# First attention: two PSUM copies move from VectorE to ScalarE, and the value bias goes into the bias row

## The reference, cut to what matters

```python
Q = (layernorm(x) @ Wq.T + bq)   # 16 heads of 8
K = (ctx @ Wk.T + bk)
V = (ctx @ Wv.T + bv)
attn = softmax(Q K^T / sqrt(8))
x = x + tanh(g_xattn[0]) * ((attn @ V) @ Wo.T + bo)
```

## Time and profile before

| what | value |
|---|---|
| median of 3 runs | 825.99 us |
| span of the profiled execution, first to last instruction | 815.2 us |
| what lies around that span, against the median | 10.8 us |
| first attention, first to last instruction | about 10.3 to 206 us |
| busy over the span: PE, DVE, ACT, POOL | 775.3, 622.4, 558.0, 476.5 us |
| steps n = 2 to 28 by the starts of L787 | 42.37 to 183.98 us |

### The profile page before, as it was taken

The page is one execution under the profiler, slowest core; times in us unless marked ns, Lnnn a source line. Parts: engine busy times, 40 slices in busy tenths (PEclk is TensorE's granted clock), DMA queues, the critical chain, the costliest instruction groups (busy, mean ns, idle before and its releaser), DMA issues. The chain is left out here.

```text
span 815.2 us, 30741 instructions
## 1 busy us (share of the span) xinstructions
PE 775.3 (95%) x10664; PEld 637.5 (78%) x10669; DVE 622.4 (76%) x2406; ACT 558.0 (68%) x1125; POOL 476.5 (58%) x892
## 2 busy tenths in 40 slices
PE   4999999999999989999999999999999999889995
PEld 2777877787788868888888888888888888558884
DVE  4799999998677767888888888888888888734442
ACT  1688878886455568777777777777777777447762
POOL 6645777773011156577677686676776776605554
PEclk9999999999999999999999999999999999999998
DMA  8804999800200000000000000000000000023110
GB/s 223 303 3 149 264 241 235 195 1 3 72 1 0 0 1 2 3 7 7 7 0 7 7 7 7 7 0 7 7 7 7 0 7 7 10 68 91 33 33 19
DMA packets 56157, 41.65 MB, mean 51 GB/s; under 512 B 3897, under 2 KB 51651, under 8 KB 55856
## 3 DMA queue, kind: packets, MB, share of 16 engines
q1 hardware_dynamic: 52400, 36.39, 17.8%
q0 software_dynamic: 2272, 4.27, 1.6%
q10 hardware_dynamic: 1440, 0.40, 0.4%
HBM read 18.07 MB, written 23.44 MB: 51 GB/s over the span
## 5 line engine op out<-in xcount | busy, mean ns | idle before, releaser
L1654 PE MATMUL l_pv<-l_Z,l_probs 128*128 128x129 f32 x1024 | 164.1, 284 | 0.6 <-DVE l_acc L1161 0.6
L1654 PEld LDWEIGHTS l_pv<-l_Z,l_probs 128*128 128x128 f32 x1024 | 138.4, 191 | 20.0 <-DVE l_acc L1161 4.9
L1433 POOL TENSOR_TENSOR l_qk_lo<-w,l_qk_hi 128x512 f16<-128x512 f32 x132 | 148.9, 1160 | 1.7 <-ACT l_qk_hi L1511 1.3
L1161 DVE SCALAR_TENSOR_TENSOR x_sb<-l_pv,l_inv,x_sb 128x128 f32 (+1 forms) x256 | 89.8, 351 | 35.3 <-DVE l_inv L1148 6.9
L52 PE MATMUL l_tz<-M,cT 128*128 128x512 f16 x396 | 108.0, 382 | 0.2 <-DVE l_Z L1239 0.2
L1497 ACT ACTIVATE l_probs<-l_b 128x512 f32<-128x512 f32 x128 | 72.8, 594 | 50.5 <-PE l_b L1620 50.4
L1487 ACT ACTIVATE w<-l_qk_bank 128x512 f32<-128x512 f32 x129 | 77.0, 597 | 44.1 <-PE l_qk_bank L52 42.4
L520 DVE TENSOR_REDUCE n_shared<-fold_bank 128x4 f32<-128x512 f32 x128 | 87.3, 682 | 9.5 <-PE fold_bank L735 9.3
L1138 DVE TENSOR_REDUCE l_neg_max<-l_a 128x4 f32<-128x512 f32 x132 | 85.8, 681 | 2.6 <-PE l_a L1598 2.1
L1491 ACT ACTIVATE l_qk_hi<-w 128x512 f16<-128x512 f32 x129 | 80.5, 624 | 1.1
L1502 ACT ACTIVATE l_Z<-l_tz 128x512 f32<-128x512 f32 x128 | 76.7, 599 | 3.6
(11 more groups left out here) (291 smaller groups left out, 2266.4 us busy)
## 6 DMA issues: line engine op xcount, KB each, us to landing
expert_rows<-empty_row SPq DMA_DIRECT2D x8, 2178.0 KB, 24.6
x_sb<-expert_rows SPq DMA_DIRECT2D x36, 66.0 KB, 2.1
x_sb<-in_x SPq DMA_DIRECT2D x4, 512.0 KB, 6.9
ctx_sb<-in_ctx SPq DMA_DIRECT2D x4, 512.0 KB, 8.0
w<-in_L_ffn_w SPq DMA_DIRECT2D x1, 2048.0 KB, 9.2
w_raw<-in_L_ffn_gate_w SPq DMA_DIRECT2D x1, 1408.0 KB, 9.6
w_raw<-in_L_ffn_up_w SPq DMA_DIRECT2D x1, 1408.0 KB, 12.2
downT<-in_L_ffn_down_w SPq DMA_DIRECT2D x2, 512.0 KB, 4.3
```

The costliest lines, as they stand in the source:

```text
L1161: nc.vector.scalar_tensor_tensor(out=total, in0=O[:, h, 0:P], scalar=inv[:, j:j + 1], in1=total, op0=ALU.mult, op1=ALU.add).then_inc(summe ...
L1433: nc.gpsimd.tensor_tensor(qk_lo[:, w, m, Q * u:Q * u + Q].rearrange("p t n -> p (t n)"), qk[:, u, m, :], qk_hi[:, w, m, Q * u:Q * u + Q].r ...
L1654: last = nc.tensor.matmul(pv_bank[m % 2][:, h * (P + 1):(h + 1) * (P + 1)], probs[:, 2 * m + h, :], Z[:, w, 2 * m + h, :], start=True, sto ...
```

## The change

Two of VectorE's calls of each step go to ScalarE: `values(n)` (a PSUM read of 128 x 128, there with an addition of the bias, now a plain Copy) stands between the stacked queries and `projected_hi`, and `heads_transposed(n-2)` stands between the stacked keys and `sums_out`. The bias `bv` is no longer added to the values: it is loaded as a column, widened to a square, multiplied by `wo0` once on TensorE, and added to the bias row. The wait of `values` on qk_hi becomes a wait on `qk_done`.

```diff
-    k.bv0 = sb("bv0", [P, P])
+    k.bv0 = sb("bv0", [P, 1])
...
-                act.dma_start(k.bv0[:, :], on_all(A["L0_xattn_bv"])).then_inc(k.bias_landed, 16)
+                act.dma_start(k.bv0[:, :], column(A["L0_xattn_bv"])).then_inc(k.bias_landed, 16)
...
+        bv_wide = heads_out
...
                 def prime():
                     dve.wait_ge(k.bias_landed, BIAS_LOADS)
-                    nc.vector.tensor_scalar(bias_row[:, :], k.bo[:, 0, :], k.tg[:, 0:1], None, ALU.mult).then_inc(primed, 1)
+                    nc.vector.tensor_copy(bv_wide[:, :], k.bv0[:, :].broadcast_to([P, P])).then_inc(bv_ready, 1)
                     nc.vector.memset(neg_max[:, :, :], 0.0).then_inc(primed, 1)
                     nc.vector.memset(V[:, :, :, :], 1.0).then_inc(primed, 1)
+                    dve.wait_ge(bv_projected, 1)
+                    nc.vector.scalar_tensor_tensor(out=bias_row[:, :], in0=k.bo[:, 0, :], scalar=k.tg[:, 0:1], in1=b_bank[0][:, 0:P],
+                                                   op0=ALU.mult, op1=ALU.add).then_inc(primed, 1)
                     dve.wait_ge(primed, 7)
...
-                def values(n, s, beside):
-
-                    dve.wait_ge(v_done, n + 1)
-                    if beside:
-                        dve.wait_ge(qk_hi_ready, 2 * n + 8)
-                    nc.vector.tensor_tensor(V[:, s % 2, :, 0:D0], front_bank[:, P:2 * P].rearrange("p (h d) -> p h d", h=H),
-                                            k.bv0[:, :].rearrange("p (h d) -> p h d", h=H), ALU.add).then_inc(V_ready, 1)
-
...
-                def heads_transposed(n):
-                    dve.wait_ge(heads_moved, n + 1)
-                    nc.vector.tensor_copy(headsT[:, :], misc_bank[:, P:2 * P]).then_inc(headsT_ready, 1)
...
                         maxima(n + 1, s + 1, 2)
-                    if live(0):
-                        values(n, s, live(3))
                     if live(3):
                         projected_lo(n + 3, s + 3)
                     if live(1):
                         maxima(n + 1, s + 1, 3)
-                    if live(-2):
-                        heads_transposed(n - 2)
...
-                        pool.wait_ge(primed, 5)
+                        pool.wait_ge(primed, 7)
...
+                def values(n, s, beside):
+                    act.wait_ge(v_done, n + 1)
+                    if beside:
+                        act.wait_ge(qk_done, n + 4)
+                    if s == 0:
+                        act.wait_ge(primed, 7)
+                    nc.scalar.activation(V[:, s % 2, :, 0:D0], front_bank[:, P:2 * P].rearrange("p (h d) -> p h d", h=H), ACT.Copy).then_inc(V_ready, 1)
+
+                def heads_transposed(n):
+                    act.wait_ge(heads_moved, n + 1)
+                    nc.scalar.activation(headsT[:, :], misc_bank[:, P:2 * P], ACT.Copy).then_inc(headsT_ready, 1)
+
...
                         stacked(n + 2, s + 2, 0, q_stacked, stack_q)
+                    if live(0):
+                        values(n, s, live(3))
                     if live(3):
                         projected_hi(n + 3, s + 3)
...
                         stacked(n + 2, s + 2, 1, k_stacked, stack_k)
+                    if live(-2):
+                        heads_transposed(n - 2)
                     if live(-1):
                         sums_out(n - 1)
...
+                pe.wait_ge(bv_ready, 1)
+                nc.tensor.matmul(b_bank[0][:, 0:P], bv_wide[:, :], k.wo0[:, :], start=True, stop=True).then_inc(bv_projected, 1)
                 every_step(pe, step)
```

More of the change, by code:

```diff
@@ L434, in first_attention @@
         names = ("primed bn_done stats_ready norm_step xn_ready cT_hi_ready cT_ready bias_added T_moved T_hi_ready T_lo_ready qk_done qk_hi_ready "
-                 "qk_lo_ready v_done V_ready q_stacked k_stacked stack_q stack_k scored max_ready maxT_moved maxT_ready shifted "
+                 "qk_lo_ready v_done V_ready bv_ready bv_projected q_stacked k_stacked stack_q stack_k scored max_ready maxT_moved maxT_ready shifted "
                  "exp_done pv_done sums_ready sums_moved inv_ready heads_ready heads_moved headsT_ready projected x_done tokens_landed w_hi_ready").split()
         (primed, bn_done, stats_ready, norm_step, xn_ready, cT_hi_ready, cT_ready, bias_added, T_moved, T_hi_ready, T_lo_ready, qk_done, qk_hi_ready,
-         qk_lo_ready, v_done, V_ready, q_stacked, k_stacked, stack_q, stack_k, scored, max_ready, maxT_moved, maxT_ready, shifted,
+         qk_lo_ready, v_done, V_ready, bv_ready, bv_projected, q_stacked, k_stacked, stack_q, stack_k, scored, max_ready, maxT_moved, maxT_ready, shifted,
          exp_done, pv_done, sums_ready, sums_moved, inv_ready, heads_ready, heads_moved, headsT_ready, projected, x_done, tokens_landed, w_hi_ready) = map(sem, names)
```

## The result

The changed kernel takes **833.46 us** in the median of five runs (830.51 to 835.05), the kernel before 825.99 (824.17 to 828.72) beside it: a ratio of 1.0084, interval [1.0061, 1.0107]. It is slower, by 7.5 us where 2.8 were forecast.

A forecast was written before the change was run, and what follows sets the result against it. Chain B through ScalarE's queue was to set the first attention's period, 5.52 us against 5.38. Periods 2.9, jumps 0, ends -0.2 and start 0.1 sum to +2.8 on the median 825.99: 828.8 us, range 825.2 to 833.6.

The forecast's parts named there:

- the forecast's own: Range of the likeliest case, 827.3 to 831 us, from the copies' bounds and the ends; +1.7 to +5 had chance 0.45.
- the dear copies: Rival: values and heads cost 0.25 us each on ScalarE, chain B 5.70, +7.3 us, 833.3; chance 0.17.
- chain B: First attention, L744 through ScalarE's queue and VectorE back to L744: 5.20 us by itself, 5.52 with both copies.
- The five jumps: Periods where the hardware loop jumps back: 5.64 to 5.71 us as now, cost 0, between -0.2 and +0.7.
- Taken as 0.16 from one row of another stage: Each new ScalarE copy's spacing, from L1875; L647's 0.25 us was the upper end.
- 0.18 us: Slack in chain B between the stacked keys and L660, where the heads' 0.16 us was to fit.
- The rival in which VectorE was the bound: Faster: the 0.30 us idle before L787 vanishes in each step, 826.0 - 7.8 = 818.2 us; chance 0.20.
- 21 ordinary periods x 0.14 = +2.9: First attention's periods without a loop jump: each grows from 5.38 to 5.52 us, +2.9 in all.
- Ends of the stage: First attention before step 2 and behind step 28: pauses and shorter hand-overs, -0.2 us, between -0.7 and +0.3.
- 10.8 us around: Median 825.99 us against the profiled span of 815.2; gave a predicted span near 818.0.
- Start, +0.1: POOL waits for VectorE's longer `prime`, with batches TensorE needs queued behind: 0 to +0.2 us, taken as +0.1.
- the cover of 1.1 us for the new matmul: At the start, behind eight warm-up matmuls, TensorE idle until 15.08; uncovered it would cost about 0.5 us.

The follow-up runs named there:

- The extra copy in the chain and in the pause: Changed kernel plus one spare ScalarE Copy per step, behind the values (chain) or behind `transposed_hi` (pause): 836.62 us, 1.0123, and 831.33 us, 1.0068, against the kernel before.
- the swap: Changed kernel with VectorE doing `add_to_x` ahead of `transposed_lo`: 826.56 us, ratio 1.0004 to the kernel before.
- the values alone: Changed kernel with the copy of the transposed heads back on VectorE, only the values on ScalarE: 825.87 us, ratio 1.0001 to the kernel before.
- one copy with the chain cut: Changed kernel with the heads back on VectorE and `add_to_x` ahead of `transposed_lo`: 821.33 us, ratio 0.9940 to the kernel before.
- the heads alone: Kernel before with only the transposed heads' copy moved to ScalarE, values and bias on VectorE: 827.01 us, ratio 1.0022.

## Why the prediction came out as it did

The direction and the mechanism of the period were right, the size was too small: +2.8 us forecast, 5.2 in known places, 5.4 and 7.5 between the medians. 833.46 lies at the upper end of the range (825.2 to 833.6) and above the forecast's own (827.3 to 831). That it lies inside is in part luck: the range reached so far for the dear copies, which are not what happened.

- **The chain.** It was forecast that the period would be set by chain B through ScalarE's queue, 5.52 against 5.38. It is 5.56 in 19 of the 21 ordinary periods; the first two take 5.63 and 5.68, where before they took 5.48 and 5.49. The extra copy in the chain and in the pause shows the queue, the swap shows the chain's last link. The five jumps were forecast at 5.64 to 5.71 and came at 5.65 to 5.66 (before: 5.67 to 5.72).
- **The copies.** Taken as 0.16 from one row of another stage; their spacing is 0.15 and 0.16. The strided destination and the extra waits cost nothing that shows. The rival with dear copies has about the right total, 833.3, by a wrong mechanism.
- **The slack.** That one of the two copies would fit in 0.18 us is shown by the values alone. The rival in which VectorE was the bound falls with it: VectorE has 11.9 us less to do in 136, and gets it back as idle time before L505. The rule that it went by (the Trainium skill, Perfetto Trace Analysis, Optimizing Scalar/DVE Operations: offloading to ScalarE may make sense where VectorE is saturated) held here for one copy with the chain cut, 0.9940, and not for two with the chain closed, 1.0084.
- **The term mis-sized first: 21 ordinary periods x 0.14 = +2.9.** The rows gave +3.63 over all 26: 19 x 0.18 and 0.34 in the first two, less 0.13 in the jumps. Of the 0.18, ScalarE's own distance grew by 0.10, less than the 0.14 forecast. The forecast took L642 to L501 as 0.31, as the earlier trace rows have it; with both copies on ScalarE `transposed_hi` lasts 0.35 instead of 0.27, and the distance is 0.38. A spacing is what a row costs its own engine, a duration what it costs the engine that waits for it; the forecast had priced the copies in chain B by the first alone.
- **The step that failed: "Ends of the stage", -0.2.** They cost +1.5. I had looked for what gets shorter when ScalarE has room, not at what is queued behind the last `heads_transposed` (four folded copies, +0.77; the heads alone show it), and the rows of before held nothing to foresee that `add_to_x` would fall in behind a blocked L359 (+0.76). The first could have been read: the edit moves a waiting copy ahead of L683 in the queue.
- **"10.8 us around" the span** was wrong: it set one execution's span against the median of others. Where the profiled execution's own time is given, 1.7 to 1.8 us lie around the span. About 10 of the difference are the last stage, which is short in that execution and in those on the chip where the kernel before takes 814.9. It changed nothing in the sum, which was added to the median, but the span forecast from it, 818.0, means nothing.
- **Start, +0.1, and the cover of 1.1 us for the new matmul:** the matmul was not covered. VectorE stood 0.24 to 0.94 us before the new bias row in the eight profiles that have it, and POOL behind it 0.29 to 0.99. What of it reaches step 2 can't be told, nor, within 2 us, whether the rise of TensorE's clock is moved by the change.

## What to carry over

A busy share names no bound: look for the closed chain through the in-order queues, add up its distances, and find its slack before adding to it. Here the first copy of 0.15 us was free, the second cost its full length in every step, and a third cost all or nothing by its place. When work moves to an engine, check what then stands between its result and whoever waits; exchanging two independent instructions on the waiting engine may be worth more than the move. And look at the last turn by itself: what waits there holds up what was never queued behind it before.

## What the runs showed that was not expected

- With both copies on ScalarE, the rows behind the stacked keys last longer: the 128 x 128 copy 0.33 to 0.35 us for 0.27, the 128 x 512 one 0.66 for 0.60, with nearly the same 0.16 and 0.48 to the next start. Why is not shown.
- A VectorE operation of 0.16 us took 1.07 beside POOL's `affine_select`, and another of 0.17 took 0.95, and only where they started behind the start of its second select.
- TensorE's rows drop from 0.31 to 0.22 us between about 25 and 37 us in the span, and not at the same time in two executions of one kernel. Six of twelve profiles record a granted clock of 0.50 in the stretch of the long rows, the others 1.00 throughout. In one (the copy in the pause) the rate rose near 22, fell near 28 and rose again near 35.
- The last stage takes 107.5 to 107.7 us on one chip and 118.3 to 118.5 on another: over 10 us, more than the effect that was measured.
